# LayerNorm statistics moved from ScalarE to VectorE's bn_stats, and the first LayerNorm woven into the mask loop

## The reference

```python
x = L0_attn_data                      # (2, 4096, 4096)
# "attention" is a block-masked linear layer
block_mask = mask.reshape(128, 32, 128, 32).sum(axis=(1, 3)) > 0
w_masked   = weight * repeat(repeat(block_mask, 32, 0), 32, 1)
x = x + layernorm(x) @ w_masked.T
# base linear layer plus 8 LoRA experts of rank 16, the best 2 chosen by a router
z = layernorm(x)
probs = softmax(z @ W_router.T);  top 2, normalised to sum 1 -> combine
h  = einsum('nd,erd->ner', z, A) * combine[:, :, None]
x  = x + z @ W_base.T + b_base + einsum('ner,eor->no', h, B) * 2.0
```

## Time and profile before

| what | value |
|---|---|
| median of 3 runs | 1850.69 us (1849.49 to 1941.23) |
| the profiled execution: device time | 1849.8 us |
| its span on the slowest core | 1848.2 us |
| spans of the 8 cores | 1832.5 to 1848.2 us |
| PE busy | 1042.4 us (56%) |
| VectorE (DVE) busy | 871.5 us (47%) |
| ScalarE (ACT) busy | 128.4 us (7%) |

### The profile page before, as it was taken

How to read it: one execution, slowest core, us unless ns; L and a number is a source line. 1 busy time by engine, 2 the same in 40 slices (tenths; PEclk the granted TensorE clock), 3 DMA queues, 4 the chain that set the end, 5 groups by cost and what they waited for, 6 DMA issues and landing times.

```text
span 1848.2 us, 23991 instructions; the slowest of 8 cores (1832.5 to 1848.2 us)
## 1 busy us (share of the span) xinstructions
PE 1042.4 (56%) x8874; PEld 868.0 (47%) x8874; DVE 871.5 (47%) x4656; ACT 128.4 (7%) x90; POOL 32.2 (2%) x48
## 2 busy tenths in 40 slices
PE   0000001000086877678787675000699999999998
PEld 0000000000075766567676564000388888888886
DVE  3556662111889999999999981112301010010101
ACT  1000000433000000000000001443000000000000
POOL 0000000000000000000000000000000000000000
PEclk9999999999998988888898888555799999999999
DMA  9998860333422222332222301234634536353541
GB/s 237 280 285 289 299 247 12 57 68 69 68 47 46 47 46 49 77 60 47 46 47 48 75 17 23 45 69 74 109 69 93 114 71 136 69 124 83 106 100 46
DMA packets 107919, 179.95 MB, mean 97 GB/s; under 512 B 68234, under 2 KB 84762, under 8 KB 103706
## 3 DMA queue, kind: packets, MB, share of 16 engines
q0 software_dynamic: 19792, 77.67, 23.2%
q1 hardware_dynamic: 88010, 100.74, 18.2%
HBM read 222.48 MB, written 16.78 MB: 129 GB/s over the span
## 4 chain that ended last, share of the span: by engine, by line
PE 42%; DVE 24%; DMA 23%; ACT 6%; issue 2%; SPq 1%; DVEq 0%; ACTq 0%; POOLq 0%
PE pp L541 25%; DVE wts L318 17%; PE pp L364 13%; DMA wts<-mask_in 11%; DMA wts<-wta 6%; DMA xnt<-xstg 6%; DVE ost L193 4%; ACT xnt L252 3%; ACT xnt L255 3%; PE pp L555 1%; PE pp L549 1%; DVE xstg L270 1%; SPq L125 1%; PE pp L458 1%; DMA r<-bp_l 1%
## 5 line engine op out<-in xcount | busy, mean ns | idle before, releaser
L364 PE MATMUL pp<-wts,xnt 128*128 128x256 bf16 x4096 | 481.9, 284 | 335.5 <-DVE wts L318 335.5
L364 PEld LDWEIGHTS pp<-wts,xnt 128*128 128x128 bf16 x4096 | 415.4, 102 | 401.9 <-issue 339.4
L318 DVE TENSOR_SCALAR wts<-wts,r 128x32 bf16<-128x32 bf16 x4096 | 565.0, 228 | 51.2 <-DMA wts<-wta 50.3
L541 PE MATMUL pp<-wts,xnt 128*128 128x256 bf16 x4096 | 460.1, 276 | 3.2 <-DVE hwt L515 3.2
L541 PEld LDWEIGHTS pp<-wts,xnt 128*128 128x128 bf16 x4096 | 404.7, 99 | 56.3 <-issue 3.5
L571 DVE TENSOR_TENSOR ost<-pp,xres 128x256 f32<-128x256 f32 x128 | 43.9, 415 | 471.2 <-PE pp L555 471.2
L193 DVE TENSOR_REDUCE ost<-wts 128x128 bf16<-128x4096 int32 x32 | 141.4, 4420 | 102.7 <-DMA wts<-mask_in 102.7
L205 PE MATMUL pp<-ost,bd_sb 128*4 128x128 bf16 x32 | 8.5, 265 | 242.8 <-DVE ost L193 242.8
L205 PEld LDWEIGHTS pp<-ost,bd_sb 128*4 128x4 bf16 x32 | 2.6, 80 | 244.6 <-issue 244.6
L252 ACT ACTIVATE xnt<-xres 128x4096 bf16<-128x4096 bf16 x16 | 57.9, 3616 | 817.7 <-DVE xres L332 692.8
L257 DVE TENSOR_SCALAR scr<-s1s 128x1 f32<-128x1 f32 x16 | 2.5, 153 | 211.2 <-ACT xnt L255 211.0
(11 more groups left out here) (48 smaller groups left out, 142.5 us busy)
## 6 DMA issues: line engine op xcount, KB each, us to landing
wts<-mask_in SPq DMA_DIRECT2D x32, 2048.0 KB, 11.9
wts<-wta POOLq DMA_DIRECT2D x16, 2048.0 KB, 12.9
wts<-wtb POOLq DMA_DIRECT2D x16, 2048.0 KB, 15.1
y_out<-ost SPq DMA_DIRECT2D x16, 1024.0 KB, 14.5
xres<-x_in POOLq DMA_DIRECT2D x8, 1024.0 KB, 18.1
r<-at_l POOLq DMA_DIRECT2D x1, 1024.0 KB, 9.4
r<-bp_l POOLq DMA_DIRECT2D x1, 1024.0 KB, 9.8
packed<-bmt_sb SPq DMA_DIRECT2D x32, 1.0 KB
```

What stands on the lines that cost most here:

```text
L318: last = vop(lambda v, kt=kt, j=j, b=b, s=s: v.tensor_scalar(wts[:, b, kt, 32 * j:32 * (j + 1)], wts[:, b, kt, 32 * j:32 * (j + 1)], mexp1 ...
L364: f = (lambda t, kt=kt, tt=tt, b=b, bank=bank, c0=c0, st=st: t.matmul(bank[:, c0:c0 + slab_n], xnt[:, tt, kt, :], wts[:, b, kt, :], start= ...
L541: top(lambda t, kt=kt, tt=tt, b=b, bank=bank: t.matmul(bank[:, 256 * (tt % 2):256 * (tt % 2) + slab_n], xnt[:, tt, kt, :], wts[:, b, kt, : ...
```

## The change

- **Statistics.** The two ScalarE passes and the four one-column VectorE steps go. In their place VectorE runs 8 `bn_stats` of 512 columns each and one `bn_aggr`, which give mean and variance. Square root, reciprocal, negated product and apply stay; their small tiles come in pairs now (`bn_buf`, `mv_buf`, `sd_buf`, `ri_buf`, `nm_buf`).
- **LayerNorm 1 in the mask loop.** For token tile t the `bn_stats` stand behind mask tile 8+2t, square root, reciprocal and apply behind mask tile 11+2t, and the transpose behind mask tile 13+2t. Staging alternates between `xstg` and the part of `xnt` that belongs to token tile 7. The first transpose waits for all x loads.
- **Mask loads.** Even tiles stay on SyncE, odd tiles go to ScalarE's queue.
- **Small copies in the mask tail.** Copy kt now waits for copy kt-1 to have landed, and matmul kt for copy kt alone.
- **LayerNorm 2.** The statistics of tile t+1 stand ahead of the apply of tile t, and the staging alternates between `xstg` and `ost`.

```diff
@@ mask loop
+            qs = (i % 2 == 0)
+            lst = RY if qs else RA
+            sem = sM0 if qs else sM1
-            c_mload.append(dma(RY, (sM0 if i % 2 == 0 else sM1), mview[i % 2],
+            c_mload.append(dma(lst, sem, mview[i % 2],
                                m2d[128 * i:128 * (i + 1), :], waits=w))
...
+            if i >= 8 and i % 2 == 0 and (i - 8) // 2 < n_tt:
+                tt = (i - 8) // 2
+                wbn = [(sXc, c_xcast[tt])]
+                pb = tt % 2
+                for j in range(D // 512):
+                    vop(lambda v, tt=tt, j=j, pb=pb: v.bn_stats(
+                        bn_buf[pb][:, 6 * j:6 * (j + 1)],
+                        xres[:, tt, 512 * j:512 * (j + 1)]),
+                        waits=(wbn if j == 0 else ()), selfw=(j == 0),
+                        tick=(j == D // 512 - 1))
+                ln1_aggr[tt] = vop(lambda v, pb=pb: v.bn_aggr(mv_buf[pb][:], bn_buf[pb][:]))
+            if i >= 13 and (i - 13) % 2 == 0 and (i - 13) // 2 < n_tt:
+                tt = (i - 13) // 2
+                w = [(pV, ln1_ap[tt])]
+                if tt == 0:
+                    w.append((sXc, c_xcast_all))
+                ln1_xb[tt] = xbar((sB0 if tt % 2 == 0 else sB1),
+                                  xnt[:, tt, :, :], ln1_src(tt), waits=w)
+            if i >= 11 and (i - 11) % 2 == 0 and (i - 11) // 2 < n_tt:
+                tt = (i - 11) // 2
+                ln1_sqrt[tt] = emit_ln_sqrt(tt, ln1_aggr[tt],
...
+                ln1_ap[tt] = vop(lambda v, tt=tt, pb=pb: v.tensor_scalar(
+                    ln1_src(tt), xres[:, tt, :], ri_buf[pb][:], nm_buf[pb][:],
+                    op0=ALU.mult, op1=ALU.add), waits=wap)
@@ mask tail
-        for kt in range(NKT):
-            c_asm.append(dma(RY, sAsm, bmTw[:, NB * kt:NB * (kt + 1)],
-                             bmt_sb[4 * kt:4 * (kt + 1), :],
-                             waits=([(pV, v_bmt)] if kt == 0 else ())))
         t_mex, v_mex = [], []
         for kt in range(NKT):
+            w = [(pV, v_bmt)] if kt == 0 else [(sAsm, c_asm[kt - 1])]
+            c_asm.append(dma(RY, sAsm, bmTw[:, NB * kt:NB * (kt + 1)],
+                             bmt_sb[4 * kt:4 * (kt + 1), :], waits=w))
             bank = pp[3 + (kt % 2)]
-            w = [(sAsm, 16 * NKT)]
+            w = [(sAsm, c_asm[kt])]
@@ LayerNorm 2
+        emit_ln2_bn(0)
         for tt in range(n_tt):
+            if tt + 1 < n_tt:
+                emit_ln2_bn(tt + 1)
+            a_sd = emit_ln_sqrt(tt, ln2_aggr[tt])
...
+            wap = []
+            if tt >= 2:
+                wap.append(((sB0 if tt % 2 == 0 else sB1), ln2_xb[tt - 2]))
+            ln2_ap[tt] = vop(lambda v, tt=tt, pb=pb: v.tensor_scalar(
+                xstg_ln2[pb], xres[:, tt, :], ri_buf[pb][:], nm_buf[pb][:],
+                op0=ALU.mult, op1=ALU.add), waits=wap)
```

More of the change, by code:

```diff
@@ L196, in _red @@
                         axis=AX.X, op=ALU.add)
-            v_red.append(vop(_red, waits=[((sM0 if i % 2 == 0 else sM1), c_mload[i])]))
+            v_red.append(vop(_red, waits=[(sem, c_mload[i])]))
             bank = pp[i % 2]
@@ new lines, in build_core_program @@
+            if i >= 13 and (i - 13) % 2 == 0 and (i - 13) // 2 < n_tt:
[8 more added lines that the diff above has]
+                ln1_sqrt[tt] = emit_ln_sqrt(tt, ln1_aggr[tt],
+                                            extra=([(sSm, c_small)] if tt == 0 else ()))
+                pb = tt % 2
+                vop(lambda v, pb=pb: v.reciprocal(ri_buf[pb][:], sd_buf[pb][:]),
+                    waits=[(pA, ln1_sqrt[tt])])
+                vop(lambda v, pb=pb: v.tensor_scalar(
+                    nm_buf[pb][:], mv_buf[pb][:, 0:1], ri_buf[pb][:], -1.0,
+                    op0=ALU.mult, op1=ALU.mult))
+                wap = []
+                if n_tt < 8:
+                    if tt >= 1:
+                        wap.append(((sB0 if (tt - 1) % 2 == 0 else sB1), ln1_xb[tt - 1]))
+                elif tt >= 2:
+                    wap.append(((sB0 if tt % 2 == 0 else sB1), ln1_xb[tt - 2]))
+                if tt == 7 and n_tt >= 8:
+                    wap.append((sB0, ln1_xb[6]))
+                ln1_ap[tt] = vop(lambda v, tt=tt, pb=pb: v.tensor_scalar(
+                    ln1_src(tt), xres[:, tt, :], ri_buf[pb][:], nm_buf[pb][:],
+                    op0=ALU.mult, op1=ALU.add), waits=wap)
@@ L219, in build_core_program @@
+        for tt in range(n_tt):
+            assert ln1_xb[tt] is not None, "LN1 schedule did not fit the mask loop"
+        ln1_b0, ln1_b1 = dcnt.get(sB0, 0), dcnt.get(sB1, 0)
         v_bmt = vop(lambda v: v.tensor_copy(bmt_sb[:], pp[2][:, 0:NB]),
@@ L247, in build_core_program @@
             c_dm = dma(RG, sAt, d_csw, csw[:, 0:2048], waits=wdm)
[L248 to L291, removed]
@@ L305, in build_core_program @@
+            c_dm = dma(RG, sAt, d_xnt, xnt[:].rearrange("p a b c -> p (a b c)"),
+                       waits=[(sB0, ln1_b0), (sB1, ln1_b1)], max_dma_last_dim=4096)
+            dbg_pre_attn = c_dm
         t_slab = []
@@ L408, in build_core_program, with emit_ln2_bn @@
                     waits=_wl, max_dma_last_dim=4096)
-        ln2_ap, ln2_xb = [], []
-        for tt in range(n_tt):
-            w = [(pV, v_attn_done), (pT, t_attn_done)]
-            if debug and tt == 0:
-                w.append((sAt, c_x2e))
-            if tt >= 1:
-                w.append(((sB0 if (tt - 1) % 2 == 0 else sB1), ln2_xb[tt - 1]))
-            ln2_ap.append(emit_ln(tt, 2, w))
+        ln2_ap = [None] * n_tt
+        ln2_xb = [None] * n_tt
+        ln2_aggr = [None] * n_tt
+        def emit_ln2_bn(tt):
+            pb = tt % 2
+            wbn = [(pV, v_attn_done), (pT, t_attn_done)]
+            if debug and tt == 0:
+                wbn.append((sAt, c_x2e))
+            for j in range(D // 512):
+                vop(lambda v, tt=tt, j=j, pb=pb: v.bn_stats(
+                    bn_buf[pb][:, 6 * j:6 * (j + 1)],
+                    xres[:, tt, 512 * j:512 * (j + 1)]),
+                    waits=(wbn if (j == 0 and tt <= 1) else ()), selfw=(j == 0),
+                    tick=(j == D // 512 - 1))
+            ln2_aggr[tt] = vop(lambda v, pb=pb: v.bn_aggr(mv_buf[pb][:], bn_buf[pb][:]))
+        emit_ln2_bn(0)
+        for tt in range(n_tt):
+            if tt + 1 < n_tt:
+                emit_ln2_bn(tt + 1)
+            a_sd = emit_ln_sqrt(tt, ln2_aggr[tt])
+            pb = tt % 2
+            vop(lambda v, pb=pb: v.reciprocal(ri_buf[pb][:], sd_buf[pb][:]),
+                waits=[(pA, a_sd)])
+            vop(lambda v, pb=pb: v.tensor_scalar(
+                nm_buf[pb][:], mv_buf[pb][:, 0:1], ri_buf[pb][:], -1.0,
+                op0=ALU.mult, op1=ALU.mult))
+            wap = []
+            if tt >= 2:
[3 more added lines that the diff above has]
+                op0=ALU.mult, op1=ALU.add), waits=wap)
             w = [(pV, ln2_ap[tt]), (pT, t_attn_done)]
@@ L420, in build_core_program @@
                 w.append((sW1, dcnt.get(sW1, 0)))
[L421 to L422 removed]
+            ln2_xb[tt] = xbar((sB0 if tt % 2 == 0 else sB1),
+                              xnt[:, tt, :, :], xstg_ln2[tt % 2], waits=w)
         ln2_b0, ln2_b1 = dcnt.get(sB0, 0), dcnt.get(sB1, 0)
```

40 lines of the change are left out of this document (25 added, 15 removed).

## The result

The changed kernel takes 1698.6 us (median of 10 runs) against 1851.2 before: ratio 0.9174, interval [0.9159, 0.9188]. Forecast was 1708, in a range of 1676 to 1752. The profiled execution took 1693.6 us for a span of 1692.0 on its slowest core, core 6 (before it was core 2). Ratios leave out slow executions, most of them in a slower state of half the chip, and medians do not; for the run `e8_ln2_act` further down these were half of six, so its time is given by its ratio.

The account below looks back on a forecast made before the run. No engine bounds the whole: loads bound the mask loop, VectorE attention; LayerNorm is a serial ring. 1849.8 less 76 (LayerNorm 2) less 66 (LayerNorm 1, net of mask loop +50, tail +20) gives 1708 us, range 1676 to 1752.

Parts of the forecast that it names:

- the reduction's rate and the fixed part of L332: LayerNorm 2: one `bn_stats` taken as 0.533 us for columns plus 0.077 fixed, 0.61 us, 4.9 for eight.
- SyncE's hold of 4.8 us: LayerNorm 2's end: transpose 6 holds SyncE 4.8 us, so transpose 7 is issued at 61.4 and lands at 68.1.
- 151.2 + 4.8 + 7: Mask loop, start of tile 14: last x load lands at 151.2, transpose holds SyncE 4.8, mask load needs 7 us.
- VectorE at 18.1 and the DMA engines at 19.5: Mask loop, tiles 14 to 27: us per pair of mask tiles for each party; 19.5 taken, seven pairs 136.5.
- The 1 to 2 us added for statistics and odd loads: Mask loop: 1 us for statistics at tiles 8 to 12 and one for odd loads, ending at 322 to 323.
- a hold of SyncE much over 4.8 us: Mask loop and LayerNorm 2: transposes holding SyncE much longer than 4.8 us would show the forecast wrong.
- I take 0.25: Mask tail: SyncE needs 0.25 us to see a copy land, atop 1.63 each; 32 x 1.88 = 60 us.
- my signs of being wrong: Pairs over 23 us, transposes holding SyncE much over 4.8 us, or stages that keep their code changing length.
- B: Both LayerNorms: `bn_stats` takes two passes, 1.14 us each, 9.5 a tile; time 1765 us; chance 0.07.
- C: Mask loop: a transpose among copies blocks the queue, nothing overlaps, pair 38.7 us; 1862, slower than before; chance 0.03.
- D: Better than thought: transposes fill idle DMA time, `bn_stats` is fast; 1680 us or below; chance 0.07.
- A: Mask loop: loads and transposes collide, pair 23.2 (26 us longer), x lands 10 us later; 1744 us; chance 0.17.

Follow-up runs that it names:

- e8_ln2_act: The changed kernel with the applies of LayerNorm 2 on ScalarE instead of VectorE; ratio 0.9136, about 1690 us.
- e11_early: The changed kernel without the first transpose's wait for all x loads and with LayerNorm 1 woven in 4 mask tiles earlier; 1738.9 us, ratio 0.9374.
- e4_no_xall: The changed kernel without the first transpose's wait for all loads of x; 1704.1 us, ratio 0.9190.

## Why the prediction was right

**LayerNorm 2** came out as worked: the eight `bn_stats` take 4.85 us, forecast 4.9 from the reduction's rate and the fixed part of L332. The pace is 7.6 instead of 7.3 because `bn_aggr` takes 0.37 us (forecast 0.2) and the waits between the small steps are a little longer. That is most of the 3 us by which the stage fell short of 76. The forecast that SyncE's hold of 4.8 us delays the last transpose held: it was issued 4.96 us behind the one before (1113.71 to 1118.67), though its apply had ended at 1115.8.

**The mask loop** ends at 320.5, forecast 322 to 323, and this closeness is in part luck: its errors cancel.

- Tile 14 starts at 167.5, forecast 166. The terms that I gave, 151.2 + 4.8 + 7, make 163. In the trace x lands 4 us earlier (147.4) and the load of tile 14 takes 14.9 us, not 7.
- The seven pairs to tile 28 take 129.4 us, forecast 136.5. I had VectorE at 18.1 and the DMA engines at 19.5 and took the larger. In the five pairs that carry statistics the pace is VectorE's, 18.67 (18.1 left out part of `bn_aggr` and of the short waits). The last two pairs carry none, which I had not seen, and take 36.0 us together. So the size was near and the party was the wrong one; the trace shows that the DMA engines need less than 19.5 a pair, and not how much less.
- Tiles 28 to 31 take 23.6 us, forecast 18.5, because I numbered the tiles one too low. The reductions in the earlier trace rows are those of tiles 13, 15, 29 and 31, and the earlier trace rows is tile 14: the earlier trace rows counts 29 VectorE instructions up to 152.00, 14 reductions with their compares and the one that starts at 151.06. Before, tile 28 started at 247.84, so that stretch took 24.8.
- The 1 to 2 us added for statistics and odd loads have no counterpart in the trace.

I had named a hold of SyncE much over 4.8 us as a sign of being wrong, and it came: 7.7 to 11.4 us for the transposes from 186 us on and 15.7 for the second one. The forecast survives it because up to tile 24 the hold is hidden under VectorE's work, with 1.1 to 1.7 us to spare; only the last, 11.35 us, is on the chain. The slowest core is the late one: its tile 14 starts at 167.5, those of the other seven between 157.5 and 165.8, and they end between 307.4 and 314.8.

**The mask tail** grew by 14, not 20: the step "I take 0.25" for SyncE's notice of a landing was too large. The copies are 1.67 us apart, forecast 1.88, of which 1.60 to 1.63 is the copy, so the notice is about 0.06. That is 32 x 0.21 = 7 us. By the Trainium skill, "SBUF — State Buffer", section "The DMA setup-cost knee", the copies would have taken 64 us; they took 54, so the row was the better guide here.

**Attention** was forecast unchanged and came 6 us shorter, about half of it by which core was slowest. That a stage with unchanged code changes its length was another of my signs of being wrong, and half of it stays open. With the 6 us of the tail, the 2 of the mask loop and the 2 behind LayerNorm 2, less the 3 of LayerNorm 2, this makes, within a us, the 14 us between 142 forecast and 156 seen in the profile.

**The rivals.** B, C and D did not occur. A had two parts, both priced and neither seen: a pair of 23.2, and x landing 10 us later (it landed at 147.4, 4 us earlier than worked). The turns of three queues did show, as an uneven order of x loads and not as a later end. The mechanism of C, a transpose that holds SyncE until other transfers are through, has its like in these runs: on the slowest core of `e11_early` the two transposes that run among the x loads hold SyncE 59 and 25 us, and the run pays 40 us. I had put it beside mask loads. It is worst with an x load there too, but 15.7 us in the changed kernel and 22.7 in `e4_no_xall` came beside mask loads alone.

## What to carry to other kernels

Work taken off the path is worth what its new host has free, and that changes along a stage: of the added `bn_stats` hardly anything showed up to tile 14, where VectorE waits for loads, and everything from there on. Moving work to another engine is not the same as taking it away: the apply on ScalarE freed VectorE and lengthened the sequence of transpose and load by 2.5 us, and nothing was gained. Read the chain of waits of such a run before naming the limit. A wait that leaves an engine idle may be keeping transfers apart that slow each other; try it without, and look at every core: without the wait the mask loop ended between 306.9 and 330.0 us on the eight cores, with it between 307.4 and 320.5 (at most 323.5 in the other runs that keep the wait and the loop). Small copies chained by their landing cost 1.67 us each; make them few before making them parallel.
